# A recurrent memory kept without its zero blocks: full-array matmuls replaced by pairs of half-array tiles

## What is computed

```python
scores = jnp.einsum('bhid,bhjd->bhij', q, k) * scale        # masked, softmax over j
att_dot = jnp.einsum('bhij,bhjv->bhiv', jax.nn.softmax(scores, axis=-1), v)
sq = jax.nn.elu(q) + 1.0
att_mem = sq @ M / (sq @ jnp.swapaxes(Z, -2, -1))
sk = jax.nn.elu(k) + 1.0
M_new = M + jnp.einsum('bhld,bhlv->bhdv', sk, v)
Z_new = Z + sk.sum(axis=-2, keepdims=True)
att = gate * att_mem + (1.0 - gate) * att_dot
out = att.reshape(B, LSEG, H * DV) @ Wo
```

## Time and profile before

| | |
|---|---|
| median of 3 runs | 1138.24 us (1134.59 to 1139.97) |
| the profiled execution | 1134.37 us |
| its span | 1132.2 us |
| PE busy | 1024.0 us, 90% of the span |
| DVE, ACT, POOL busy | 778.0, 617.8, 561.6 us |
| a step, from one output projection to the next | mostly 54.4 us |

### The profile page before, as it was taken

How to read it: one execution, slowest core, us unless ns; L and a number is a source line. 1 busy time by engine, 2 the same in 40 slices (tenths; PEclk the granted TensorE clock), 3 DMA queues, 4 the chain that set the end, 5 groups by cost and what they waited for, 6 DMA issues and landing times.

```text
span 1132.2 us, 18929 instructions
## 1 busy us (share of the span) xinstructions
PE 1024.0 (90%) x7108; PEld 724.1 (64%) x7172; DVE 778.0 (69%) x1514; ACT 617.8 (55%) x1259; POOL 561.6 (50%) x685
## 2 busy tenths in 40 slices
PE   0999999998999999999999998999998889999961
PEld 0477777776777777767777776777776755333431
DVE  2769686968686868787786969696858433334465
ACT  3556565545565654556564644565656344666562
POOL 2246565535565654456565635374746332222366
PEclk9999999999999999999999999999999899999985
DMA  5100000000000000000000000000000003000015
GB/s 166 39 2 19 10 11 10 11 11 10 11 10 15 7 17 4 20 1 19 1 20 1 19 2 20 1 20 1 11 1 11 25 7 158 1 0 0 1 38 111
DMA packets 14983, 23.81 MB, mean 21 GB/s; under 512 B 5424, under 2 KB 7216, under 8 KB 14384
## 3 DMA queue, kind: packets, MB, share of 16 engines
q1 hardware_dynamic: 14252, 20.41, 6.0%
q10 hardware_dynamic: 644, 2.23, 0.7%
HBM read 13.97 MB, written 8.65 MB: 20 GB/s over the span
## 4 chain that ended last, share of the span: by engine, by line
PE 76%; ACT 9%; DVE 8%; issue 2%; DMA 2%; POOL 2%; SPq 0%; POOLq 0%; ACTq 0%; DVEq 0%
PE ps L1133 21%; PE ps L1230 11%; PE ps L1190 7%; PE ps L1340 7%; ACT arena L607 6%; PE ps L1177 4%; PE ps L1166 4%; PE ps L1196 4%; PE ps L1149 4%; PE ps L1353 3%; PE ps L1215 3%; PE ps L1202 3%; DVE arena L864 2%; PE ps L1161 2%; DMA arena<-in_L_attn_x_dram 2%
## 5 line engine op out<-in xcount | busy, mean ns | idle before, releaser
L1133 PE MATMUL ps<-arena 128*128 128x512 f16 x1152 | 267.8, 383 | 1.7 <-DVE arena L839 1.7
L607 ACT ACTIVATE arena<-ps,arena 128x128 f32<-128x128 f32 x512 | 138.9, 382 | 130.8 <-DVE arena L864 130.5
L1133 PEld LDWEIGHTS ps<-arena 128*128 128x128 f16 x1152 | 113.5, 99 | 120.9 <-issue 5.6
L839 DVE STREAM_TRANSPOSE arena<-ps 128x1024 f32<-128x1024 f32 x96 | 146.2, 1523 | 27.7 <-PE ps L1133 25.4
L438 POOL TENSOR_TENSOR arena<-arena 128x256 f32<-128x256 f32 x128 | 93.3, 729 | 133.2 <-DVE arena L883 69.5
L1190 PE MATMUL ps<-arena 128*128 128x65 f32 x1024 | 136.1, 276 | 10.4 <-ACT arena L613 4.7
L1190 PEld LDWEIGHTS ps<-arena 128*128 128x128 f32 x1024 | 128.2, 193 | 23.4 <-ACT arena L613 8.0
L781 DVE BATCH_NORM_STATS2 arena<-arena 128x6 f32<-128x256 f32 x100 | 37.0, 411 | 139.5 <-ACT arena L625 121.6
L423 POOL TENSOR_TENSOR arena<-arena 128x512 f32<-128x512 f32 x48 | 73.1, 1522 | 107.7 <-ACT arena L600 107.7
L1230 PE MATMUL ps<-arena 128*128 128x256 f32 x544 | 122.0, 382 | 0.3 <-ACT arena L619 0.3
L1230 PEld LDWEIGHTS ps<-arena 128*128 128x128 f32 x544 | 102.0, 190 | 16.1 <-ACT arena L619 1.4
(11 more groups left out here) (110 smaller groups left out, 1814.3 us busy)
## 6 DMA issues: line engine op xcount, KB each, us to landing
x_rows<-arena SPq DMA_DIRECT2D x17, 256.0 KB, 2.0
arena<-x_rows SPq DMA_DIRECT2D x4, 1024.0 KB, 7.9
out_dram<-arena SPq DMA_DIRECT2D x32, 128.0 KB, 2.8
arena<-in_L_attn_x_dram SPq DMA_DIRECT2D x62, 64.0 KB
arena<-in_L_attn_Wq_dram ACTq DMA_DIRECT2D x2, 512.0 KB, 10.9
arena<-in_L_attn_Wk_dram ACTq DMA_DIRECT2D x2, 512.0 KB, 17.0
arena<-in_L_attn_Wv_dram SPq DMA_DIRECT2D x2, 512.0 KB, 23.4
arena<-in_L_attn_Wo_dram SPq DMA_DIRECT2D x8, 128.0 KB, 6.5
```

The source lines that it names most:

```text
L607: last = act.activation(Pr[:, par, j, :], s_bank[:, par, j * P:(j + 1) * P], ACT.Exp, bias=negm[:, par, j:j + 1])
L839: dve.transpose(dst[:, d0:d0 + 32], bank.rearrange("p w (d c) -> p d w c", c=C)).then_inc(x_free, 1)
L1133: last = pe.matmul(bank[:, w, :], xc[:, lx, k, w * P:(w + 1) * P], W16[lw][:, k, i, :], start=(n == 0), stop=(n == 5))
```

## The change

The memory is kept as 128 partitions x 65 columns for two units, without the zero blocks. The read-out of the memory becomes, for each pair of units, two matmuls of 64 rows x 128 columns of weights against 65 columns (one on the lower, one on the upper 64 rows of the array), each into its own bank. The update becomes two matmuls of 128 rows x 64 columns of weights against 65 columns, whose results stand above each other in one bank. The probabilities' four matmuls write by `par` into the two banks as well. `divide` then adds or copies all 128 partitions in one instruction. The start loses POOL's memset of M, and ACT fills M with two copies.

```diff
-        M = alloc(UNITS // 2 * 2 * DV1).rearrange("p (j h e) -> p j h e", j=UNITS // 2, h=2)
+        M = alloc(UNITS // 2 * DV1).rearrange("p (j e) -> p j e", j=UNITS // 2)
...
-                pool.memset(M, 0.0).then_inc(init, 1)
...
-                act.wait_ge(init, 1)
-                for g in range(GROUPS):
-                    for par in range(2):
-                        p = slice(64 * par, 64 * par + 64)
-                        act.activation(M[p, GP * g:GP * g + GP, par, :],
-                                       M0[p, GP * g % (H // 2):GP * g % (H // 2) + GP, :],
-                                       ACT.Copy).then_inc(m_reset, 1)
+                for y in range(2):
+                    act.activation(M[:, y * HP:y * HP + HP, :], M0, ACT.Copy).then_inc(m_reset, 1)
...
-                    T = pm_bank[:, :, 4 * DV1:6 * DV1].rearrange("p j (h e) -> p j h e", h=2)
-                    for par in range(2):
-                        p = slice(64 * par, 64 * par + 64)
-                        m = M[p, j:j + 2, par, :]
-                        if s < NSEG - 1:
-                            last = dve.tensor_tensor(m, T[p, :, par, :], m, ALU.add)
-                        elif bp < PAIRS - 1:
-                            last = dve.tensor_copy(m, M0[p, j0:j0 + 2, :])
+                    m = M[:, j:j + 2, :]
+                    if s < NSEG - 1:
+                        new = pm_bank[:, 0, 4 * DV1:6 * DV1].rearrange("p (j e) -> p j e", j=2)
+                        last = dve.tensor_tensor(m, new, m, ALU.add)
+                    elif bp < PAIRS - 1:
+                        last = dve.tensor_copy(m, M0[:, j0:j0 + 2, :])
...
-                        pe.matmul(pm_bank[:, 0, u * DV1:(u + 1) * DV1], PT[:, par, j, :],
+                        pe.matmul(pm_bank[:, par, u // 2 * DV1:(u // 2 + 1) * DV1], PT[:, par, j, :],
                                   v[:, GP * (g % 2) + j, par, 0:DV1], start=True, stop=True)
...
-                        last = pe.matmul(pm_bank[:, 1, a * 2 * DV1:(a + 1) * 2 * DV1], sqT[g % 2][:, j, :],
-                                         M[:, GP * g + j, :, :], start=True, stop=True)
+                        for par in range(2):
+                            p = slice(64 * par, 64 * par + 64)
+                            last = pe.matmul(pm_bank[:, par, (2 + a) * DV1:(3 + a) * DV1], sqT[g % 2][p, j, :],
+                                             M[p, GP * g + j, :], start=True, stop=True)
...
-                            last = pe.matmul(pm_bank[:, a, 4 * DV1:6 * DV1],
-                                             sk[:, 2 * DK * (GP * (g - g % 2) + h):
-                                                2 * DK * (GP * (g - g % 2) + h + 1)], v[:, h, :, 0:DV1],
-                                             start=True, stop=True)
+                            for par in range(2):
+                                unit = 2 * (GP * (g - g % 2) + h) + par
+                                last = pe.matmul(pm_bank[64 * par:64 * par + 64, 0, (4 + a) * DV1:(5 + a) * DV1],
+                                                 sk[:, DK * unit:DK * (unit + 1)], v[:, h, par, 0:DV1],
+                                                 start=True, stop=True)
```

More of the change, by code:

```diff
@@ L109, in infini_block_kernel @@
         sqT = [alloc(GP * P).rearrange("p (j i) -> p j i", j=GP) for _ in range(2)]
-        M = alloc(UNITS // 2 * 2 * DV1).rearrange("p (j h e) -> p j h e", j=UNITS // 2, h=2)
+        xcur = [alloc(TILE, F16).rearrange("p (l k r) -> p l k r", l=2, k=KT) for _ in range(2)]
+        M = alloc(UNITS // 2 * DV1).rearrange("p (j e) -> p j e", j=UNITS // 2)
         M0 = alloc(H // 2 * DV1).rearrange("p (j e) -> p j e", j=H // 2)
@@ L115, in infini_block_kernel @@
         att = alloc(UNITS * DK)
-        xcur = [alloc(TILE, F16).rearrange("p (l k r) -> p l k r", l=2, k=KT) for _ in range(2)]
         sk = alloc(UNITS * DK)
@@ L120, in infini_block_kernel @@
         Pr = alloc(GU * P).rearrange("p (h j i) -> p h j i", h=2, j=GP)
-        AB = [alloc(2 * 4 * DK).rearrange("p (m u e) -> p m u e", m=2, u=4) for _ in range(2)]
+        AB = [alloc(2 * 4 * DK) for _ in range(2)]
         nat = alloc(2 * H * DK).rearrange("p (w e c) -> p w e c", w=2, c=C)
@@ L128, in infini_block_kernel @@
         negm = alloc(GU).rearrange("p (h j) -> p h j", h=2)
-        rr = alloc(8).rearrange("p (m u) -> p m u", m=2)
+        rr = alloc(8).rearrange("p (r u) -> p r u", r=2)
         n_st, r_st = (alloc(2 * 6).rearrange("p (w s) -> p w s", s=6) for _ in range(2))
@@ L429, in gated @@
                     n = 8 * s + 2 * g + half
-                    mem, dot = (AB[half][:, m, :, :].rearrange("p (h r) e -> p h r e", r=2) for m in (1, 0))
+                    dot, mem = (AB[half].rearrange("p (r m h e) -> p m h r e", r=2, m=2, h=2)[:, m] for m in range(2))
                     h = GP * (g % 2) + 2 * half
@@ L477, in step @@
                     gated(bp, s, 2, 1)
-                pool.wait_ge(init, 5)
+                pool.wait_ge(init, 4)
                 pool.sem_inc(att_done, 8)
@@ L868, in divide @@
                     n = 8 * s + 2 * g + half
-                    rd = pm_bank[:, :, 0:4 * DV1].rearrange("p m (u e) -> p m u e", u=4)
+                    rd = pm_bank[:, :, 0:4 * DV1].rearrange("p r (u e) -> p r u e", u=4)
                     dve.wait_ge(pm_full, bp * 32 + n + 1)
@@ L873, in divide @@
                     dve.wait_ge(att_done, bp * 32 + n + 7)
-                    last = dve.tensor_tensor(AB[half], rd[:, :, :, 0:DK],
-                                             rr.rearrange("p m (u a) -> p m u a", a=1).to_broadcast([P, 2, 4, DK]),
+                    last = dve.tensor_tensor(AB[half].rearrange("p (r u e) -> p r u e", r=2, u=4), rd[:, :, :, 0:DK],
+                                             rr.rearrange("p r (u a) -> p r u a", a=1).to_broadcast([P, 2, 4, DK]),
                                              ALU.mult)
                     j, j0 = GP * g + 2 * half, (GP * g + 2 * half) % (H // 2)
-                    T = pm_bank[:, :, 4 * DV1:6 * DV1].rearrange("p j (h e) -> p j h e", h=2)
-                    for par in range(2):
-                        p = slice(64 * par, 64 * par + 64)
-                        m = M[p, j:j + 2, par, :]
-                        if s < NSEG - 1:
-                            last = dve.tensor_tensor(m, T[p, :, par, :], m, ALU.add)
-                        elif bp < PAIRS - 1:
-                            last = dve.tensor_copy(m, M0[p, j0:j0 + 2, :])
+                    m = M[:, j:j + 2, :]
[4 more added lines that the diff above has]
+                        last = dve.tensor_copy(m, M0[:, j0:j0 + 2, :])
                     last.then_inc(pm_free, 1)
@@ L984, in step @@
                         take_x(bp, s, 5)
-                dve.wait_ge(init, 4)
+                dve.wait_ge(init, 3)
                 dve.memset(gacc, 0.0).then_inc(gs_done, 1)
@@ L1189, in read_out @@
                         j, par = 2 * half + u // 2, u % 2
-                        pe.matmul(pm_bank[:, 0, u * DV1:(u + 1) * DV1], PT[:, par, j, :],
+                        pe.matmul(pm_bank[:, par, u // 2 * DV1:(u // 2 + 1) * DV1], PT[:, par, j, :],
                                   v[:, GP * (g % 2) + j, par, 0:DV1], start=True, stop=True)
                     if bp == 0 and s == 0:
-                        pe.wait_ge(m_reset, 2 * (g + 1))
+                        pe.wait_ge(m_reset, g // 2 + 1)
                     for a in range(2):
                         j = 2 * half + a
-                        last = pe.matmul(pm_bank[:, 1, a * 2 * DV1:(a + 1) * 2 * DV1], sqT[g % 2][:, j, :],
-                                         M[:, GP * g + j, :, :], start=True, stop=True)
+                        for par in range(2):
+                            p = slice(64 * par, 64 * par + 64)
+                            last = pe.matmul(pm_bank[:, par, (2 + a) * DV1:(3 + a) * DV1], sqT[g % 2][p, j, :],
+                                             M[p, GP * g + j, :], start=True, stop=True)
                     if s < NSEG - 1:
```

## The result

The changed kernel takes 1141.13 us (median of 20 runs, 1139.28 to 1143.14) against 1137.38 us before, run beside it (20 runs, 1133.01 to 1141.08). The ratio is 1.0031, with a 95% interval from 1.0018 to 1.0044: 0.3% slower, which is clear of no change, but within the 0.5% that the prediction names as what a measurement tells from no change. 1143 us and 0.4% had been forecast. The profiled execution has a span of 1137.5 us, 5.3 above that of before.

What follows compares the result with a forecast made beforehand. PE, busy for 90% of the span, bounds the kernel. Losses of 11.2 us less gains of 6.3 give +4.9 on 1134.4, so 1139.3 us; with the profiled run 3.9 below the median, 1143 us, summed case's range 1137 to 1148.

Steps and rivals of the forecast that it cites:

- The matmuls and the switches: Each updated read-out: three array shape changes cost 0.43 us, shorter update loads save 0.22, so 0.21 us longer.
- The direct pass between tile shapes: In a read-out, from 64-row to 64-column tiles: taken as one shape change, about 0.14 us.
- two switches: Rival: going directly between tile shapes costs two shape changes, 7.4 us more over about 53 updated read-outs: 1150 us; chance 0.12.
- a free pass: Rival: going directly between tile shapes in a read-out costs nothing: 1136 us; chance 0.06.
- tiles that take turns: Rival: memory and update passes don't run in pairs, 0.67 us more per read-out, about 45 us: 1187 us; chance 0.05.
- halved loads: Rival: 64-row tiles halve the load's price, memory steps cost 0.056, each read-out 0.22 us less: 1128 us; chance 0.13.
- The path: Ordinary windows between output projections: uncovered read-outs (2,0), (3,0), (3,1), (0,0), (0,1) add 0.85 us; eight windows give 6.8 us.
- (1,1), (2,1) and (1,0): Read-outs in ordinary windows, covered by 0.39 us waits and a 0.28 us issue wait; without cover each would cost 0.21.
- The gain at the three pairs' ends: Windows from s = 3 into the next pair: one copy fewer gains 3.9 us, avoided clock falls 2.4, together 6.3.
- The copies' wait: At divide(3,0) of s = 3, three times: PE waits 1.5 us for two POOL-delayed copies; the second's 1.33 falls away.
- the last pair's end: Final pair, where PE waits up to 3.1 us for others: longer read-outs add perhaps 0.8 us.
- The falling clock: Rival: 1.2 GHz also around the two 0.4 us waits of each s = 3 step, 7 us: 1150 us; chance 0.10.

Runs made afterwards that it cites:

- the late copy: Kernel before, with the s = 3 copies of divide(3,0) left to divide(3,1), which copies four units in two instructions; matmuls stay full-array: 1129.68 us, ratio 0.9919.
- the two copies: Changed kernel with the copy of M0 split again into two instructions of 64 partitions: 1150.97 us, ratio 1.0109.
- the memory's tiles alone: Changed kernel with 29 extra matmuls in the last step, but the update as full-array matmuls of 130 columns: 1144.06 us, ratio 1.0051.
- the two kernels with extra matmuls: Changed kernel and kernel before, each with 29 extra full-array matmuls of constants in the last step: 1132.66 and 1131.99 us.

## Why the prediction was right

**The matmuls and the switches.** Pairs run together, a 128-column load lasts as long for 64 rows as for 128, and the update's loads step by 0.06: each as read from L1373 and L1360. The direct pass between tile shapes, which no row of before showed, costs one switch, 0.09 to 0.10 us behind the last streamed column. That agrees with the Trainium skill, TensorEngine Tiling (Array Packing), Key Properties, by which a change of mode drains TensorE; the speedup of up to 2x in the same page's Theoretical Speedup does not show for the memory's 64-row pairs, whose loads step by 0.11 as full ones do, while the loads of the update's 64-column pairs step by 0.06. The rivals with two switches, with a free pass, with tiles that take turns, and with halved loads are all excluded by the rows of one read-out, and the ordinary windows of 55.09 bear that out. (One reading of the prediction is loose: 1.02 less 0.599 is 0.42, not 0.43 for a pass of 512 columns. In the trace such passes do start 0.43 apart, so nothing hangs on it.)

**The path.** Ordinary windows rose by 0.69 us where 0.85 was summed. (1,1), (2,1) and (1,0) were covered, as said. The part on the path was a little too large, by 0.03 us for each of the five read-outs.

**DVE.** The gain at the three pairs' ends was 6.7 us; 6.3 less 0.9 for the read-outs beside them had been summed. The copies' wait was the right cause, as the late copy and the two copies show. Its size was put too low: without a fall of the clock a window with the wait takes 55.4 us, and in the late copy 53.4, so the wait costs 2.0 us where 1.3 was summed. A fall behind it costs 0.9 and 1.2 us in the two windows of before, where 1.2 was summed for each. But that the clock falls behind such a wait is not sure: in the profiles with the 1.5 or 1.3 us waits it fell at 10 of 15 pair ends, in those without at 1 of 21, the one behind the 0.4 us wait.

**The mis-sized term** is "the last pair's end, where PE waits up to 3.1 us for others, perhaps 0.8". It was 5.3 us in the profiled pair of executions. The falling clock had been thought of as a rival, but for the 0.4 us waits of s = 3, where the changed kernel's profile doesn't show it and only that of the memory's tiles alone does, once. That the kernel before has such falls at its end too, in some executions, could not be read from the one profile. The sum of the other steps, +7.5 - 6.7 = +0.8 us, agrees with the 0.7 between the medians of the two kernels with extra matmuls. So the forecast of 0.4% slower met 0.3% partly by chance: its losses in the steps were some 2 us too large, its gains 1 us too small, and the end made up for both. That the sum for an execution like the profiled one, 1139.3 us, meets the 1139.28 of the changed kernel's profiled execution is the same chance: the end's +5.3 us stands there where +0.8 had been summed.

## What to carry to other kernels

Zeros in a matmul cost nothing while weight loads set the pace, as here, where passes of 65 and of 130 columns both follow one another by 0.112 us: look at the start-to-start distance of passes with different column counts before removing them. In such a stream half-array tiles saved time only where the load got shorter (64 columns of weights, not 64 rows), and each change of the array's shape was paid with about 0.145 us, so put tiles of one shape together. A side effect (one copy less at a contended moment, a clock kept up over waits) can be worth more than the change, and may be had alone.

## What was not expected

A passage of little work can cost twice: once as the wait, and again by the 1.2 GHz level, which followed 10 of the 15 waits for the copies. Twenty-nine matmuls whose results nobody reads took 5.2 us off the kernel before and 8.5 off the changed one, although they only fill places where PE waits for other engines.
